# Eight images through two transformer layers: the opening written into each engine's program, and a feed-forward that works in fours

## The chip, the core and the metric

The kernel runs on one core of a Trainium2 chip. A core has five engines with instruction streams of their own, which meet only through semaphores: TensorE (PE in the profile; PEld is its weight load, PEq its sequencer), VectorE (DVE), ScalarE (ACT), GpSimd (POOL) and SyncE (SP, which only starts transfers here). SBUF is the on-chip memory with 128 partitions; PSUM holds eight banks of 512 float32 values per partition, into which PE writes. The metric is the device time of one execution, in microseconds (us).

## The reference

Eight images of 32 x 32 positions and 384 channels go through two layers. B = 8, T = 1024 tokens, C = 384, six heads of 64.

```
x = x + attention0(group_norm(x))          # 32 groups over all positions; scores + rel_h + rel_w,
                                           # from tables rel_pos_h, rel_pos_w; softmax; proj_w, proj_b
t = x as tokens
t = t + causal_attention(layer_norm(t))    # Wq, Wk, Wv, Wo, bo
h = layer_norm(t) @ kron(c_fc_1, c_fc_2).T # 384 -> 1536; c_fc_1 is 1536 x 32, c_fc_2 is 1 x 12
t = t + gelu(h) @ kron(c_proj_1, c_proj_2).T   # c_proj_1 is 32 x 1536, c_proj_2 is 12 x 1
```

Because the feed-forward weights are Kronecker products, the kernel works with 32 values per token: it sums the 384 channels in groups of 12 with c_fc_2, multiplies by c_fc_1 (the up product), takes the gelu, multiplies by c_proj_1 (the down product), and then spreads each of the 32 results over 12 channels with c_proj_2.

## The kernel before

Precision comes from pairs: most operands are split in a high float16 part and a low one, and a product is made of three float16 products (high x high, high x low, low x high). The down and spread products are float32.

**The opening** consists of three blocks of the program. At the end of a block all engines wait for one another.
- `constants` (lines 132 to 277). SP loads four small tables, c_fc_1, c_proj_1, and then eight pieces of weights through five staging buffers. ACT queues six bias loads and the first image (x to `xin`), makes the high half of each weight piece (L182), and later copies tables out of PSUM (L185, L187). DVE makes the low halves (L194). POOL writes every constant in one list of fills (L224) and carvings with affine_select (L230): identities, masks, the group matrix, the position one-hots in `ka0`, zeroed `qc` and `kc`, the spread matrix; each waits for the one before. Only after the last (L265, semaphore `shaped`) does PE start: two products for the relative tables (L272), then 24 transposes of c_proj_1 (L275) and c_fc_1 (L277).
- `first_image`. It normalises image 0: 24 transposes of x in six units (L323), copies on ACT (L328), statistics on DVE, group averages over partitions by PE (`average`, L342, nine products, once for means and once for variances), the root on POOL (L370), the scaled image on ACT (L382), its high half on ACT (L388) and its low half on POOL (L394). PE waits for all six units, then makes the q and k projections, six pairs of heads (`pair_products`, L486). ACT (L505) and DVE (L522, L527) take each pair out of PSUM. POOL then makes twelve turned copies of q (`turn`, L539), which start when the third pair is done.
- The main block, in which each engine runs its own program over the eight images.

**An image in the main block.** PE makes the values (L602, L605), with the relative products between them (L569, 64 rows by 32 columns each, on four column groups), the layer-0 attention, its output projection, the layer norm, the layer-1 projections and attention, the output projection and the feed-forward. During the layer-0 attention the next image is loaded and normalised (L323, L342, L394 between the scores). During the feed-forward PE makes the next image's q and k projections as fill.

**The feed-forward** has twelve steps per image. A step of PE is: `up` (L1218, two products, each 96 rows x 512 columns, into banks 0 and 1), `down` of the step before (L1235, two products with 128 rows and 32 output partitions, at two of four places q), six fill matmuls in steps 1 to 9 (L486), and in steps 7 to 10 a `spread` (L1253, 128 x 384, float32). ACT's gelu (L1226) must be done before the next up, since both use the same banks. ACT also takes out the next image's pairs between gelus (`HIGHS`). After the steps come four more spreads. DVE copies the down sums out (L1241) and adds each spread to x (L1257). SP stores x in two halves (L1263) and loads the next x when both have landed (L1473); POOL adds the output bias to it inside the attention (L997). PE's next values may start at once; its second group of relative products waits for all eight adds.

## Time and profile before

| | us |
|---|---|
| median of 3 runs (lowest, highest) | 3124.77 (3123.82, 3130.79) |
| the profiled execution, its own time | 3126.24 |
| span from its first to its last instruction | 3124.5 |
| PE busy, of the span | 2768.5 (89%) |
| DVE busy | 2187.7 (70%) |
| ACT busy | 1763.3 (56%) |
| POOL busy | 1767.5 (57%) |
| opening, to the first values product | 135.7 |
| image 0 in the main block, to the first values of image 1 | 380.0 |

The busy times are averages over stages with different limits, so the stages have to be read one at a time. A line of a timeline gives the start, the length, the engine, the source line, the instruction, what it writes and reads, how many such instructions are merged in it, and in brackets how long the engine had been idle and what ended that. "issue" is idle time for which no releaser shows.

### The profile page before, as it was taken

The page shows a single profiled execution, that of the slowest core. Times are in us where ns is not written, and L with a number is a line of the kernel's source. Part 1 is how long each engine was busy: PE and PEld are TensorE (multiplying, and loading weights), DVE is VectorE, ACT ScalarE, POOL GpSimd, SP SyncE. Part 2 cuts the span into 40 slices and gives each one's busy share as a digit, 9 for nine tenths or more (in the row PEclk, how much of TensorE's full clock was granted, in tenths as well). Part 3 has the DMA queues.
Part 4 walks back from the last instruction along what each step waited for, and adds up shares of the span by engine and source line. Part 5 has one row for each costly group of instructions (what it writes and reads, how often), then busy time and mean ns, then how long its engine had stood idle before and what let it go on. Part 6 is the DMA issues. An engine that isn't in the chain of part 4 may idle for free.

```text
span 3124.5 us, 68549 instructions
## 1 busy us (share of the span) xinstructions
PE 2768.5 (89%) x29084; PEld 1590.4 (51%) x29084; DVE 2187.7 (70%) x3787; ACT 1763.3 (56%) x2090; POOL 1767.5 (57%) x1166
## 2 busy tenths in 40 slices
PE   1689998999889999899988999989999899889997
PEld 1346563565536554365634556346563565535553
DVE  2476776768768686786857867677776768757684
ACT  2456555566555665565645656556556565555563
POOL 6457373664546656374653737457374574647563
PEclk9799999999999999999999999999999999999998
DMA  2000001000010000100001000100001000010000
GB/s 94 21 21 2 1 2 42 22 2 1 2 62 2 2 2 1 62 2 1 2 11 52 2 1 2 41 22 2 1 2 42 22 2 1 2 42 2 2 2 21
DMA packets 32751, 48.11 MB, mean 15 GB/s; under 512 B 5152, under 2 KB 32032, under 8 KB 32448
## 3 DMA queue, kind: packets, MB, share of 16 engines
q1 hardware_dynamic: 29904, 41.55, 4.0%
q8 instruction: 231, 3.78, 0.5%
q10 hardware_dynamic: 2544, 2.18, 0.2%
q14 instruction: 72, 0.59, 0.1%
HBM read 30.95 MB, written 12.58 MB: 14 GB/s over the span
## 4 chain that ended last, share of the span: by engine, by line
PE 47%; POOL 15%; DVE 15%; issue 12%; ACT 6%; POOLq 0%; DVEq 0%; ACTq 0%
PE ps L486 11%; POOL pl L926 8%; PE ps L812 7%; POOL ph L969 5%; PE ps L602 5%; DVE mxp L882 4%; PE ps L773 4%; PE ps L782 4%; PE ps L737 4%; DVE pl L926 3%; PE ps L1235 3%; PE ps L775 2%; DVE x L1042 2%; DVE stats L1046 2%; PE ps L1253 2%
## 5 line engine op out<-in xcount | busy, mean ns | idle before, releaser
L926 POOL TENSOR_TENSOR pl<-p,ph 128x1024 f16<-128x1024 f32 x336 | 825.2, 2456 | 402.4 <-ACT ph L859 387.4
L882 DVE TENSOR_REDUCE mxp<-ps 128x1 f32<-128x512 f32 (+2 forms) x1344 | 777.8, 626 | 188.7 <-PE ps L737 181.3
L857 ACT ACTIVATE p<-ps 128x1024 f32<-128x1024 f32 (+1 forms) x672 | 644.8, 961 | 450.8 <-PE ps L782 444.6
L812 PEld LDWEIGHTS ps<-v,ph 128*128 128x128 f16 x9600 | 516.6, 98 | 129.5 <-issue 37.6
L926 DVE TENSOR_TENSOR pl<-p,ph 128x1024 f16<-128x1024 f32 (+1 forms) x336 | 414.8, 1234 | 214.4 <-POOL ph L969 212.3
L812 PE MATMUL ps<-v,ph 128*128 128x65 f16 (+1 forms) x9600 | 540.6, 195 | 20.4 <-DVE pl L926 12.5
L812 PE MATMUL ps<-v,pl 128*128 128x65 f16 x4800 | 517.8, 194 | 0.0
L812 PEld LDWEIGHTS ps<-v,pl 128*128 128x128 f16 x4800 | 452.0, 100 | 0.0
L617 POOL TENSOR_TENSOR v<-o,v 128x384 f16<-128x384 f32 x128 | 113.5, 891 | 517.9 <-ACT o L613 517.7
L782 PE MATMUL ps<-qc,kc 65*128 65x512 f16 (+3 forms) x1344 | 388.1, 371 | 0.0
L859 ACT ACTIVATE ph<-p 128x1024 f16<-128x1024 f32 x336 | 355.6, 1058 | 10.7
L969 POOL TENSOR_SCALAR ph<-p 128x1024 f16<-128x1024 f32 (+1 forms) x336 | 331.5, 987 | 0.5 <-ACT p L857 0.2
L773 PE MATMUL ps<-qa,ka 128*128 128x512 f16 x768 | 298.4, 389 | 0.0
L775 PE MATMUL ps<-qb,ka 128*128 128x512 f16 x768 | 298.3, 388 | 0.0
L737 PE MATMUL ps<-ka,qa 128*128 128x512 f16 x768 | 250.4, 387 | 44.3 <-DVE mxp L882 34.6
L782 PEld LDWEIGHTS ps<-qc,kc 65*128 65x128 f16 (+1 forms) x1344 | 126.0, 100 | 131.0 <-issue 9.1
L612 ACT ACTIVATE v<-ps 128x384 f16<-128x384 f32 x128 | 63.7, 498 | 226.3 <-PE ps L605 152.7
L486 PE MATMUL ps<-xin,wqkv_hi 128*128 128x512 f16 x576 | 151.5, 386 | 24.1 <-DVE x L1042 12.4
L737 PE MATMUL ps<-qb,qa 128*128 128x512 f16 (+2 forms) x576 | 157.5, 328 | 15.8 <-DVE mxp L882 15.6
L737 PEld LDWEIGHTS ps<-ka,qa 128*128 128x128 f16 x768 | 73.7, 98 | 188.7 <-DVE mxp L882 90.7
L773 PE MATMUL ps<-qa,qb 128*128 128x512 f16 (+1 forms) x576 | 165.5, 350 | 0.0
L539 POOL TENSOR_SCALAR hT<-qa 64x1024 f16<-64x1024 f16 x48 | 91.5, 1917 | 125.2 <-DVE qc L527 123.5
(182 smaller groups left out, 5300.7 us busy)
## 6 DMA issues: line engine op xcount, KB each, us to landing
x<-in_x SPq DMA_DIRECT2D x8, 1536.0 KB, 7.8
out<-x SPq DMA_DIRECT2D x16, 768.0 KB, 3.8
xin<-in_x SPq DMA_DIRECT2D x7, 1536.0 KB, 6.8
xin<-in_x ACTq DMA_DIRECT2D x1, 1536.0 KB, 19.8
qc<-rowt SPq DMA_DIRECT2D x96, 2.0 KB
o<-in_L_conv_qkv_w SPq DMA_DIRECT2D x2, 576.0 KB, 11.4
p<-in_L_conv_qkv_w SPq DMA_DIRECT2D x1, 576.0 KB, 13.0
x<-in_L_attn_Wq SPq DMA_DIRECT2D x1, 576.0 KB, 13.0
```

The lines of the kernel that those rows point to most:

```text
L486: mm = nc.tensor.matmul(m.ps[:, self.bank[i] + j, :], w[:, k, self.order[i] * P:(self.order[i] + 1) * P], x(k, 4 * j, 4 * j + 4), start=(n ...
L602: mm = nc.tensor.matmul(m.ps[:, 6 + t % 2, 0:C], flat_tile(x(k, t, t + 1)), w[:, k, 2 * C:3 * C], start=(n == 0), stop=(self.layer == 1 an ...
L737: mm = nc.tensor.matmul(m.ps[:, bank, 0:w], m.qa[:, sl, qt * P:(qt + 1) * P], self.ka[:, sl, kh * BANK:kh * BANK + w], start=not diag, sto ...
L773: nc.tensor.matmul(outs[j], self.ka[:, sl, keys[j]], m.qa[:, sl, q], start=True, stop=False)
L775: nc.tensor.matmul(outs[j], self.ka[:, sl, keys[j]], m.qb[:, sl, q], start=False, stop=False)
L782: mm = nc.tensor.matmul(outs[j], m.kc[crows(h), sl, keys[j]], m.qc[crows(h), sl, q], start=False, stop=True)
L812: mm = nc.tensor.matmul(m.ps[:, 6 + half % 2, c0:c0 + w], e, v, start=(first and n == 0), stop=(g in self.last_of_half and n == len(work) ...
L857: nc.scalar.activation(m.p32[:, i % RING, :, 0:w], m.ps[:, 2 * (i % 2):2 * (i % 2) + 2, 0:w], ACT.Exp, scale=SCALE).then_inc(s["exp"], 1)
L859: self.high_part(act, i, lambda out, in_: nc.scalar.activation(out, in_, ACT.Copy), s["hi_act"])
L882: nc.vector.reduce_max(m.mxp[:, h % 2, kh, qt:qt + 1], m.ps[:, bank, 0:w], AX.X).then_inc(s["free"], 1)
L926: engine.tensor_tensor(m.pl[:, i % RING, :, 0:w], m.p32[:, i % RING, :, 0:w], m.ph[:, i % RING, :, 0:w], ALU.subtract).then_inc(sem, 1)
L969: self.high_part(pool, i, lambda out, in_: nc.gpsimd.tensor_scalar(out, in_, 1.0, 0.0, ALU.mult, ALU.add), self.s["hi_pool"])
```

## The change

The blocks of the opening go. A class `Prologue` writes it as one part at the head of each engine's program in the main block, in an order of its own:
- SP loads c_fc_1, c_proj_1, the first image, the small tables, then the weights. The biases stay on ACT's queue.
- POOL makes the identity first, then the group matrix, the small ones and the one-hots for one head of each parity (DVE copies them to the other two later); the 16-bit identities, masks and spread matrix come after the norm's low halves. Zeroing of `qc` and `kc` is cut to the halves that need it and moves to DVE.
- PE transposes c_proj_1 and c_fc_1 first, then x. c_fc_1 goes from PSUM to its place without a copy in SBUF.
- The scaling of the first image moves from ACT to DVE; its low halves are shared by POOL and DVE, and PE starts the first pair channel by channel. Weight halves are put between the steps of ACT and DVE.
- The turned copies are made pair by pair: for image 0, those of the high parts on ACT and those of the low parts on POOL; for later images all on POOL, from the first finished pair on.
- `average` leaves out products of the group matrix whose block is zero: seven products instead of nine, for every image.

The feed-forward works in fours: `down` does four products at the four places q, every second step, behind the fill. The spread matrix becomes 128 x 32 (it sums the four places), so that `spread` gives 32 values per token; it is issued once per half image (after step 8 and at the end). DVE multiplies them out to 384 channels with c_proj_2 (`widen`, two tiles each), and POOL adds the result to x. The next image's values wait for the first two widenings, and its second group of relative products for all four.

```diff
-class Stage:
...
+    def sync(self, sp):
+        d, s = self.d, self.s
+        sp.sem_inc(self.stored, STORES)
+        sp.dma_start(self.c1in, d.c_fc_1.rearrange("(i p) a -> p i a", p=P)).then_inc(s["ffn_in"], 16)
+        sp.dma_start(self.cpin, d.c_proj_1).then_inc(s["ffn_in"], 16)
+        sp.dma_start(self.m.xin[:, :, :], d.x_tiles[0]).then_inc(s["first_in"], 16)
+        for i, r in enumerate((d.rel_h, d.rel_h, d.rel_w, d.rel_w)):
+            sp.dma_start(self.rel2[:, i, :], r).then_inc(s["rel_in"], 16)
+        for i, (src, _, _) in enumerate(self.pieces):
+            if i >= self.NS:
+                sp.wait_ge(s["lo_done"], i - self.NS + 1)
+            sp.dma_start(self.stage[i % self.NS], src).then_inc(self.loads[i % self.NS], 16)
+        sp.wait_ge(s["lo_done"], len(self.pieces))
...
+        act.wait_ge(s["cp_mm"], NF)
+        nc.scalar.activation(m.cp[:, :, :], m.ps[:, 4, 0:NF * FA].rearrange("p (a b) -> p a b", a=NF), ACT.Copy).then_inc(s["cp_out"], 1)
+        act.wait_ge(s["c1_mm"], NF)
+        for r in range(2):
+            nc.scalar.activation(m.c1[r * FA:(r + 1) * FA, :], m.ps[0:FA, 1:4, :].rearrange("p a b -> p (a b)"), ACT.Copy).then_inc(s["c1_hi"], 1)
+        for n in range(2 * NC_):
+            act.wait_ge(norm.s["transposed"], norm.s.at("transposed", n + 1))
+            norm.copy(act, n, n)
+        for i in range(self.NS):
+            self.weight_high(act, i)
+        for n in range(2 * NC_):
+            norm.high(act, n)
+        act.wait_ge(s["biases_in"], 16 * 6)
+        for i in range(2 * NPAIR):
+            if self.NS + i < len(self.pieces):
+                self.weight_high(act, self.NS + i)
+            qkv.pair_high(act, i)
+            if i < NPAIR:
+                for parity in range(2):
+                    act.wait_ge(qkv.s["hi"], qkv.s.at("hi", 2 * i + parity + 1))
+                    dst, src = qkv.turned(0, i, parity)
+                    nc.scalar.activation(dst, src, ACT.Copy).then_inc(qkv.s["turned_hi"], 1)
+        act.wait_ge(s["lo_done"], len(self.pieces))
...
+        dve.wait_ge(s["c1_hi"], 2)
+        nc.vector.tensor_tensor(m.c1[2 * FA:3 * FA, :], m.ps[0:FA, 1:4, :].rearrange("p a b -> p (a b)"), m.c1[0:FA, :], ALU.subtract).then_inc(s["c1_lo"], 1)
+        for n in range(2 * NC_):
+            dve.wait_ge(norm.s["copied"], norm.s.at("copied", n + 1))
+            norm.stats(dve, n, n).then_inc(norm.s["stats"], 1)
+            if n % 2 == 1:
+                dve.wait_ge(norm.s["stats"], norm.s.at("stats", n + 1))
+                norm.aggregate(dve, n // 2)
+        for i in range(2):
+            self.weight_low(dve, i)
+        dve.wait_ge(norm.s["mean_mm"], norm.s.at("mean_mm", 1))
+        norm.mean_out(dve, 6).then_inc(norm.s["mean_out"], 1)
+        dve.wait_ge(norm.s["mean_out"], norm.s.at("mean_out", 1))
+        norm.deviations(dve)
+        self.weight_low(dve, 2)
+        self.weight_low(dve, 3)
+        dve.wait_ge(norm.s["var_mm"], norm.s.at("var_mm", 1))
+        norm.eps(dve, 7).then_inc(norm.s["var_eps"], 1)
+        norm.shifts(dve)
+        dve.wait_ge(norm.s["shift"], norm.s.at("shift", 1))
+        for n in range(2 * NC_):
+            norm.normalise_dve(dve, n)
+            if n % 2 == 1:
+                norm.low_dve(dve, n)
...
+        for i in range(2 * NPAIR):
+            if 4 + i < len(self.pieces):
+                self.weight_low(dve, 4 + i)
+            qkv.pair_low(dve, i)
+        dve.wait_ge(s["ka_made"], 1)
+        for h in (0, 1):
+            for p in (1, 2):
+                nc.vector.tensor_copy(m.ka0[other(h), slot(h) + p, :], m.ka0[other(h), slot(h), :])
...
+        fill(m.ident[:, :], 0.0)
+        carve(m.ident[:, :], ALU.not_equal, 1.0, 0, [[-1, P]], 1, "ident_made")
+        fill(m.group[:, :, :], 1.0 / GC)
...
+        pool.wait_ge(norm.s["var_eps"], norm.s.at("var_eps", 1))
+        norm.root(pool)
+        for n in range(0, 2 * NC_, 2):
+            norm.low(pool, n)
...
+        for i in range(NPAIR):
+            pool.wait_ge(qkv.s["lo"], qkv.s.at("lo", 2 * i + 2))
+            for parity in range(2):
+                qkv.turn(pool, 1, i, parity)
...
+        pe.wait_ge(s["ident_made"], 1)
+        pe.wait_ge(s["ffn_in"], 32)
+        for i in range(NF):
+            nc.tensor.transpose(m.ps[:, 4, i * FA:(i + 1) * FA], self.cpin[:, i * P:(i + 1) * P], m.ident[0:FA, 0:FA]).then_inc(s["cp_mm"], 1)
+        for i in range(NF):
+            nc.tensor.transpose(m.ps[0:FA, 1 + i // 4, (i % 4) * P:(i % 4 + 1) * P], self.c1in[:, i, :], m.ident[:, :]).then_inc(s["c1_mm"], 1)
+        pe.wait_ge(s["first_in"], 16)
+        for n in range(2 * NC_):
+            if n == 1:
+                pe.wait_ge(s["c1_lo"], 1)
+                pe.wait_ge(s["c1_hi"], 2)
+            if n == 4:
+                pe.wait_ge(s["cp_out"], 1)
+            norm.transposes(pe, n, n).then_inc(norm.s["transposed"], 1)
+        pe.wait_ge(s["group_made"], NC_)
+        norm.means(pe, 6).then_inc(norm.s["mean_mm"], 1)
+        norm.variances(pe, 7).then_inc(norm.s["var_mm"], 1)
+        pe.wait_ge(s["anti_made"], 1)
+        pe.wait_ge(s["rel_in"], 64)
+        for i in range(2):
+            nc.tensor.matmul(m.ps[:, 5, i * NREL:(i + 1) * NREL], self.rel2[:, 2 * i:2 * i + 2, :].rearrange("p a b -> p (a b)"), self.anti,
+                             start=True, stop=True).then_inc(s["rel_mm"], 1)
+        pe.wait_ge(s["lo_done"], NC_)
+        for i in range(2 * NPAIR):
+            if i == 1:
+                pe.wait_ge(s["rel_out"], 1)
+            qkv.pair_products(pe, i, channel_ready=norm.ready if i == 0 else None)
+        pe.wait_ge(s["lo_done"], len(self.pieces))
+        pe.wait_ge(s["made"], 1)
+        pe.wait_ge(s["const_dve"], 1)
...
+            near = [k for k in range(NC_) if abs(k - i) <= 1]
+            for k in near:
                 mm = self.nc.tensor.matmul(self.m.ps[:, bank, i:i + 1], self.m.group[:, k, i * P:(i + 1) * P], value(k),
-                                           start=(k == 0), stop=(k == NC_ - 1))
+                                           start=(k == near[0]), stop=(k == near[-1]))
...
+    def turn_all(self, pool):
+        s = self.s
         for p in range(NPAIR):
-            op = self.nc.gpsimd.tensor_scalar(dst[rows, p, :].rearrange("p (w h) -> p w h", w=IMG),
-                                              src[rows, parity * NPAIR + p, :].rearrange("p (h w) -> p w h", h=IMG), 1.0, 0.0, ALU.mult, ALU.add)
-        op.then_inc(self.s["turned"], 1)
-        if n == 3:
-            pool.wait_ge(self.s["turned"], self.s.at("turned", 4))
+            pool.wait_ge(s["lo"], s.at("lo", 2 * p + 2))
+            for part in range(2):
+                for parity in range(2):
+                    self.turn(pool, part, p, parity)
+        pool.wait_ge(s["turned_lo"], s.at("turned_lo", NH))
...
-    BANKS = (6, 6, 6, 6, 0, 1, 0, 1)
-    COUNTS = dict(scaled=8, summed=8, offset=2, x2=8, x2_t=2, x2_hi=4, x2_lo=2, up=12, act=12, each=12, o2=2, spread=8, added=8)
+    BANKS = (6, 0)
+    COUNTS = dict(scaled=8, summed=8, offset=2, x2=8, x2_t=2, x2_hi=4, x2_lo=2, up=12, act=12, each=6, o2=2, spread=2, widened=4, added=8)
...
-    def down(self, pe, i):
+    def down(self, pe, n):
         m, s = self.m, self.s
-        hf, f = i // self.PAIRS, 2 * (i % self.PAIRS)
-        pe.wait_ge(s["act"], s.at("act", i + 1))
-        for j in range(2):
-            q = (f + j) % 4
-            mm = self.nc.tensor.matmul(m.ps[q * FA:(q + 1) * FA, 6 + hf, :], m.cp[:, f + j, :], m.p32[:, i % self.NHID, j, :],
-                                       start=(f + j < 4), stop=(f + j >= NF - 4), skip_group_check=True)
+        hf, f = 2 * n // self.PAIRS, 4 * n % NF
+        pe.wait_ge(s["act"], s.at("act", 2 * n + 2))
+        for q in range(4):
+            mm = self.nc.tensor.matmul(m.ps[q * FA:(q + 1) * FA, 6 + hf, :], m.cp[:, f + q, :], m.p32[:, (2 * n + q // 2) % self.NHID, q % 2, :],
+                                       start=(f == 0), stop=(f == NF - 4), skip_group_check=True)
...
-    def spread(self, pe, t):
-        if t % 4 == 0:
-            pe.wait_ge(self.s["o2"], self.s.at("o2", t // 4 + 1))
-        if t in (1, 2, 3):
-            pe.wait_ge(self.s["added"], self.s.at("added", t))
-        elif t in (4, 5):
+    def spread(self, pe, hf):
+        pe.wait_ge(self.s["o2"], self.s.at("o2", hf + 1))
+        if hf == 1:
             pe.wait_ge(self.s["act"], self.s.at("act", 2 * self.PAIRS))
-        elif t >= 6:
-            pe.wait_ge(self.s["added"], self.s.at("added", t - 1))
-        self.nc.tensor.matmul(self.m.ps[:, self.BANKS[t], 0:C], self.o2[:, t * P:(t + 1) * P], self.m.spread[:, :], start=True, stop=True).then_inc(self.s["spread"], 1)
-    def add(self, dve, t):
-        dve.wait_ge(self.s["spread"], self.s.at("spread", t + 1))
-        self.nc.vector.tensor_tensor(self.m.x[:, t, :], self.m.ps[:, self.BANKS[t], 0:C], self.m.x[:, t, :], ALU.add).then_inc(self.s["added"], 1)
+        for t in range(4 * hf, 4 * hf + 4):
+            mm = self.nc.tensor.matmul(self.m.ps[:, self.BANKS[hf], t % 4 * FA:(t % 4 + 1) * FA], self.o2[:, t * P:(t + 1) * P], self.m.spread[:, :], start=True, stop=True)
+        mm.then_inc(self.s["spread"], 1)
+    def widened(self, n):
+        buf = self.m.ph if n % 2 == 0 else self.m.pl
+        return flat(buf[:, 2:4, :, :].rearrange("p r a b -> p r (a b)")).bitcast(F32)[:, 0:2 * C].rearrange("p (t a b) -> p t a b", t=2, b=FB)
+    def widen(self, dve, n):
+        hf, t = n // 2, 2 * (n % 2)
+        dve.wait_ge(self.s["spread"], self.s.at("spread", hf + 1))
+        if hf == 1:
+            dve.wait_ge(self.s["added"], self.s.at("added", 2 * (n - 1)))
+        y = self.m.ps[:, self.BANKS[hf], t * FA:(t + 2) * FA].rearrange("p (t a) -> p t a", a=FA)
+        self.nc.vector.tensor_tensor(self.widened(n), y.unsqueeze(3).broadcast_to([P, 2, FA, FB]),
+                                     self.m.cp2[:, :].unsqueeze(1).unsqueeze(1).broadcast_to([P, 2, FA, FB]), ALU.mult).then_inc(self.s["widened"], 1)
+    def add(self, pool, n):
+        pool.wait_ge(self.s["widened"], self.s.at("widened", n + 1))
+        x = self.m.x[:, 2 * n:2 * n + 2, :]
+        self.nc.gpsimd.tensor_tensor(x, self.widened(n).rearrange("p t a b -> p t (a b)"), x, ALU.add).then_inc(self.s["added"], 2)
...
+                if before and t == 0:
+                    pe.wait_ge(before.ff.s["widened"], before.ff.s.at("widened", 2))
                 qkv0.v_products(pe, t)
                 for n in WITH_V[t]:
                     if n == 0:
                         pe.wait_ge(qkv0.s["lo"], qkv0.s.at("lo", 2 * PAIRS))
                     if before and n == 1:
-                        pe.wait_ge(before.ff.s["added"], before.ff.s.at("added", NT))
+                        pe.wait_ge(before.ff.s["widened"], before.ff.s.at("widened", 4))
...
-                if i >= 1:
-                    ff.down(pe, i - 1)
                 if i < 2 * ff.PAIRS and FILL[i] and w.next:
                     after.fill(pe, 3 * EACH + sum(FILL[:i]), 3 * EACH + sum(FILL[:i + 1]))
-                if i in SPREADS:
-                    ff.spread(pe, SPREADS.index(i))
-            for t in range(4, NT):
-                ff.spread(pe, t)
+                if i >= 2 and i % 2 == 0:
+                    ff.down(pe, i // 2 - 1)
+                if i == 8:
+                    ff.spread(pe, 0)
+            ff.spread(pe, 1)
...
-            for t in range(4):
-                ff.add(dve, t)
-                if t in (1, 2):
-                    low(4, (t - 1,))
+            low(4, (0,))
+            ff.widen(dve, 0)
+            ff.widen(dve, 1)
+            low(4, (1,))
             low(5, (0,))
             ff.o2_out(dve, 1)
-            ff.add(dve, 4)
-            ff.add(dve, 5)
             low(5, (1,))
-            ff.add(dve, 6)
-            ff.add(dve, 7)
+            ff.widen(dve, 2)
+            ff.widen(dve, 3)
...
-                for n in range(4):
-                    w.next.qkv0.turn(pool, n)
+                w.next.qkv0.turn_all(pool)
+            for n in range(4):
+                ff.add(pool, n)
```

## Rows read from the trace of the kernel before

**Rows 1.** busy time per stage (us): length, then PE, PEld, DVE, ACT, POOL, clock, DMA
```profile
0.00:135.68 135.68, 42.47 (x196) 26.11 (x196) 40.30 (x52) 37.58 (x41) 81.99 (x65) 0.88 0.17 54
...
477.00:515.66 38.66, 37.73 (x140) 11.44 (x139) 14.96 (x18) 19.71 (x19) 22.87 (x12) 0.92 0.06 21
```

**Rows 2.** timeline of the constants, POOL (start us, length us)
```profile
27.19 2.99 POOL L230 TENSOR_SCALAR_AFFINE_SELECT ident<-ident 128x128 f32<-128x128 f32 x2 [0.24 <-POOL kc L224]
...
55.66 0.14 POOL L265 MEMSET small<- 128x48 f32 x1
```

**Rows 3.** the same timeline, weights and feed-forward tables on ACT, DVE, PE
```profile
18.69 1.17 ACT L182 ACTIVATE wqkv_hi<-p 128x1152 f16<-128x1152 f32 x1 [0.86 <-DMA p<-in_L_conv_qkv_w]
...
30.14 1.36 DVE L194 TENSOR_TENSOR wo_lo<-p,wo_hi 128x1152 f16<-128x1152 f32 x1
...
58.32 2.74 PE L277 MATMUL ps<-ident,pl 128*32 128x128 f32 x12
...
61.09 1.44 ACT L187 ACTIVATE lT<-ps 32x1536 f32<-32x1536 f32 x1 [2.18 <-PE ps L277]
...
64.51 1.75 DVE L207 TENSOR_TENSOR c<-lT,c 32x1536 f16<-32x1536 f32 x1
```

**Rows 4.** the same timeline, norm of the first image
```profile
68.52 5.17 PE L323 MATMUL ps<-ident,xin 128*128 128x128 f32 x24 [7.46 <-PEq L132]
...
75.40 2.77 PE L342 MATMUL ps<-gmv,group 128*128 128x1 f32 x18 [1.72 <-DVE gmv L335]
...
79.08 4.00 PE L342 MATMUL ps<-small,group 128*128 128x1 f32 x18 [0.91 <-DVE small L360]
...
84.47 0.81 ACT L382 ACTIVATE hT<-xin,small 128x512 f32<-128x512 f32 x1 [10.15 <-DVE small L374]
...
94.09 1.89 PE L486 MATMUL ps<-xin,wqkv_hi 128*128 128x512 f16 x4 [11.01 <-POOL xin L394]
...
99.74 2.25 ACT L505 ACTIVATE qa<-ps,bqk 64x1024 f16<-64x1024 f32 x2 [6.93 <-PE ps L486]
```

**Rows 5.** timeline, end of the first projections, POOL and PE
```profile
123.71 11.49 POOL L539 TENSOR_SCALAR lT<-qb 64x1024 f16<-64x1024 f16 x6
...
135.73 0.48 PE L602 MATMUL ps<-wqkv_hi,xin 128*128 128x384 f16 x1 [15.68 <-PEq L400]
```

**Rows 6.** DMA issues: times, KB each, median us from issue to landing
```profile
xin<-in_x SPq DMA_DIRECT2D x7, 1536.0 KB, 6.8
xin<-in_x ACTq DMA_DIRECT2D x1, 1536.0 KB, 19.8
```

**Rows 7.** chain of waits in the first feed-forward (start us, length us)
```profile
477.62 1.85 PE ps L1235 x4
...
485.39 0.43 PE ps L1218 x2
485.82 0.98 PE ps L1235 x4
486.81 1.40 PE ps L486 x6
...
506.40 0.65 PE ps L1253 x2
...
514.27 1.56 PE ps L1253 x4
...
517.55 1.13 PE ps L569 x96
518.68 1.57 PE ps L602 x9
```

**Rows 8.** timeline of PE, group means inside the attention
```profile
244.18 2.17 PE L342 MATMUL ps<-gmv,group 128*128 128x1 f32 x18
```

**Rows 9.** one line of POOL: durations ns min, median, max
```profile
L997 POOL TENSOR_TENSOR x<-x,bo x72: 986/994/6696, 184.0 to 2951.5; 128x384 f32<-128x384 f32 x64, 128x3072 f32<-128x3072 f32 x8
```

**Rows 10.** one line of DVE: durations ns min, median, max
```profile
L1257 DVE TENSOR_TENSOR x<-ps,x x64: 548/558/559, 500.2 to 3120.0; 128x384 f32<-128x384 f32 x64
```

352 lines of the change are left out of this document (152 added, 200 removed).

## The prediction

> **What bounds the kernel now.** I read the busy time by stage first, then the timeline of the opening, then the chain of waits through one feed-forward. The first 135.7 us are the opening, once per run: PE works for 42.5 us of it and POOL for 82.0 [rows 1]. The timeline says why. POOL writes every constant in one list and releases PE only after the last one, at 55.8 us, though the identity matrices that the transposes need were carved from 27.2 on, 2.99 for two [rows 2]. Then three blocks run one behind the other: tables, the first norm (from 68.5), the first projections (from 94.1) [rows 4]. The last block ends with POOL's turns, 123.71 + 11.49 = 135.2, and PE, which waited 15.7 us at the block's end, starts the values at 135.73 [rows 5].
>
> After that the bound is PE. In the feed-forward stage of an image with a next one, PE is busy 37.7 of 38.7 us [rows 1], and the chain of waits runs on PE alone: up 0.43, down 0.98, fill 1.40, one after the other, 2.81 a step [rows 7]. What leaves this stage leaves the run, seven times (the eighth image has no fills).
>
> **The opening, step by step.** SP now issues c_fc_1, c_proj_1, x, then the small tables and weights.
> (a) The two feed-forward tables land at about 8 us, and x (issued near 2 us) at about 13. The bounds for x are its landing alone, 6.8 us after issue, and crowded, 19.8 [rows 6]: 9 to 22. I take 13, since the weights now queue behind it.
> (b) PE turns the tables: 2.74 for twelve transposes [rows 3], about 4.2 for all 24 (the other twelve are narrower). ACT copies twice, 2 x 1.44, and DVE subtracts, 1.75 [rows 3]. 8 + 4.2 + 2.9 + 1.8 = 17 us. The second unit of the norm waits for this, so the tables, not x, set the pace. POOL's identity needs only a fill and about 1.4 [rows 2].
> (c) The second unit was at 68.5 + 5.17/6 = 69.4 and the scale was ready at 84.47 [rows 4]: 15.1 us. Each average now has 7 products for 9: 2/9 of 2.77 + 4.00 is 1.5 off. ACT puts five weight halves (1.17 each) and DVE four (1.36 each) between these steps [rows 3]; they fit beside PE's averages except about 1.5. Ready at 17 + 15.1 = 32.
> (d) From the scale to the end of the first pair took 99.74 - 84.47 = 15.3 us, 9.6 of it until all six units were ready [rows 4]. The norm is now split over DVE, ACT and POOL, and the products start channel by channel. I take 10.5: 42.5.
> (e) From there to the values took 135.73 - 99.74 = 36.0 [rows 4, 5]. POOL's turns behind the third pair go: half are POOL's, per pair and in cover of the later pairs, half go to ACT. ACT's load for a q pair is 2.25 + 1.17 + two turns [rows 3, 4]; a turn has 1024 elements as one of the two in the 2.25 has, so 1.1 each, bounded above by POOL's 11.49/6 = 1.9 [rows 4, 5]. That is 5.6 a pair, then three k pairs with PE waiting for banks, about 23 with the last DVE half, and then DVE's four copies, the sum and the bias halves, some 3, while PE waits; with sequencing and bank waits I take 29.5. Values start at 72.
> Saved: 135.7 - 72 = 64. Bounds: 54 (x at 22 costs 5, turns at 1.9 cost 5) to 72 (tables and x sooner by 4, no blocking, 2 less at the end).
>
> **The feed-forward, per image.** Downs: twelve pairs of matmuls at 0.98 [rows 7]. A pair of 128 x 32 products already takes hardly longer than one: it should be near 1.7 one behind the other, as 384 columns of such a product take 0.65 [rows 7] and 512 would take 0.87. Four in four different column groups: nothing in the trace has four with 128 rows. The nearest row is the relative products, which put 96 products of 96 columns on four column groups in 1.13 us, where one by one, at the up's 0.43 for 1024 such columns, they would take 3.9 [rows 7]. So I take 1.0 for a group of four, with 1.97 (two pairs) as the other end: 12 x 0.98 - 6 x 1.0 = 5.8.
> The Trainium skill, TensorE: Matmul & The Clock Gate, section on packing small matmuls, gives 2.38 times for three column tiles rather than 3. By that ratio four would cost about 1.1 and the saving would be 5.2; no row here shows it.
> Spreads: eight of 384 columns, four at 0.65 in the loop and four at 1.56/2 behind it, 5.7 [rows 7]. Now eight of 32 columns. The nearest rows are products of one column, 18 records in 2.17, 0.12 each, two records a product [rows 8]: 8 x 0.24 = 1.9. Upper end the old price. Saved 3.8.
> Given back: behind the shorter loop ACT (gelu and half a high part a step) is late for the last up: the last gelu waits for a high part, and PE idles about 1.6. Net 5.8 + 3.8 - 1.6 = 8.0.
> DVE had eight adds at 0.56 [rows 10], and has four widenings of 768 elements, about 1.0 each, two in the loop, two under the next image's values. The adds go to POOL: 384 elements 0.99, 3072 elements 6.70 [rows 9], so 768 take 1.8. They hide: the turns, 23 us of POOL, start earlier, per pair, and the last two adds lie under the next image's first products; the reload of x comes 2 to 3 us later against those products and is first needed inside the attention. Behind POOL's last adds, which wait for DVE's widening, stand only the value low halves, and PE needs those no sooner than its first weighted values. New waits of PE: the first values for the first two widenings (long done), the second group of relative products for all four, some 2 us behind the spread and under the first values. Uncovered, the last two adds would cost 3.6.
> The clock: at the start of the loop, after PE had waited for the first gelus, a pair of downs ran at 1.85 for 0.98, TensorE's lower level [rows 7]. The new end of the loop has idles of 1.6 and 0.8 with little between them. If it falls there, the next values and relative products (1.57 + 1.13 [rows 7]) take up to 2.4 more. I count half, 1.2: 6.8 net, x 7 = 48. Bounds a image: 2.2 (no four-way overlap) to 9.
> **The averages inside the attention.** Four products fewer per next image, on a PE that does not pause there: 8 records x 0.12 = 0.9 [rows 8], x 7 = 6. If another engine sets the pace there, 0.
> **The last image.** Its steps wait for ACT, so the downs give nothing; four spreads leave the loop (about -2), and the tail gets POOL's adds (1.8 for 0.56, twice): 0, within 3.
>
> **Sum.** 64 + 48 + 6 = 118. Against the profiled execution, 3126.24 (span 3124.5): 3008. The median of the runs, 3124.77, is 1.5 below it, which I leave in the range.
>
> **The rivals.**
> *Four tiles don't overlap.* For it: only pairs are seen with 128 rows. Against: the relative products, 3.5 times faster than one by one. The downs then save nothing: 64 + 7 x 2.2 + 6 = 85, 3041. Chance 0.12.
> *The opening stays serial.* Each engine runs one program in order, so a late weight holds the norm behind it (ACT's copies of five weights ahead of the first high part). If weights (31.5, the end of the last low half [rows 3]), tables 12, norm 24 and projections 30 still add, values start near 98 and it saves 38: 3034. Against it: identity and tables need none of the weights. Chance 0.12.
> *The feed-forward's gain is given back to the next image.* The values now wait for DVE's widening and the stores for POOL. If these take it all: 64 + 6, 3056. Against: DVE works 15.0 of 38.7 us and POOL 22.9 [rows 1]. Chance 0.07.
> *Slower: the clock stays low.* With one down in two steps PE may idle enough to sit at 1.2 GHz for the whole stage. That stage keeps some 30 us of full-speed work, so +30 an image, 210 in all, against 118: 3218. It decides from 118/7 = 17 us an image at the lower level. Against: the fills keep PE at work in nine steps. Chance 0.03.
>
> **How the numbers follow.** The forecast, 3008 (own range 2988 to 3030), has 0.66. I put the range from 2990 to 3042: it takes in the first two rivals and the bounds of the opening. The measurement tells 0.2%, 6 us, from nothing; no case lies within it but a mixture, 0.01. Faster 0.96, slower 0.03.
>
> **What would show it.** The first values near 72 us (right: 62 to 82), x's landing before 14, ACT's turns at 1.1. Four downs in about 1.0 us and not 1.9; spreads at 0.24; a stage, from the second up to the next values, shorter by 6 to 9 us; values at 0.16 us apart (full clock) or 0.32. An image's period shorter by 7 to 8 us. Wrong if x lands past 22, if DVE's ordered list waits on a late weight, or if periods do not shrink.

## The result and the profile after

The changed kernel takes 3034.96 us (median of 4 runs, 3029.49 to 3037.59) against 3127.68 us for the kernel before on the same chip (3123.82 to 3130.79): ratio 0.9702, 95% interval 0.9682 to 0.9721. Its profiled execution took 3037.59 us with a span of 3035.9. I had forecast 3008, with a range from 2990 to 3042: faster as forecast, within the range, 27 us (30 on the profiled execution) short of the forecast itself.

All lines below are of the profiles named, and line numbers are those of the kernel in question; in the changed kernel L327 and L329 are the table transposes, L400 the transposes of x, L501 the low halves of the scaled image, L547 the pairs, L566 their copies on ACT, L583 and L588 on DVE, L205 and L602 the turns on ACT and POOL, L671 the values, L1286, L1302 and L1316 up, down and spread, L1331 the widening and L1337 the wide addition.

Busy time by stage, changed kernel (columns as in [rows 1]); the opening and the first stage with fills:

```profile
0.00:77.34 77.34, 44.31 (x188) 24.81 (x188) 53.05 (x66) 45.27 (x42) 38.01 (x48) 0.86 0.38 116
408.30:446.91 38.61, 32.50 (x167) 12.75 (x166) 23.96 (x24) 26.64 (x27) 26.77 (x14) 0.93 0.06 21
```

The opening is 58.3 us shorter (135.7 to 77.4), with about the same work of PE in it (44.3 against 42.5) and POOL's work down from 82.0 to 38.0. Its timeline, PE, DVE and ACT in turn, against [rows 3 to 5]:

```profile
8.58 1.45 PE L327 MATMUL ps<-ident,p 32*128 32x32 f32 x12 [8.58 <-DMA p<-in_L_ffn_c_proj]
...
14.96 1.11 PE L400 MATMUL ps<-ident,xin 128*128 128x128 f32 x4 [2.25 <-DMA xin<-in_x]
...
17.49 4.26 PE L400 MATMUL ps<-ident,xin 128*128 128x128 f32 x20 [1.41 <-DVE c L216]
...
31.27 0.16 DVE L452 SCALAR_TENSOR_TENSOR small<-small 128x3 f32<-128x3 f32 x1 [1.05 <-POOL small L448]
...
34.60 1.87 PE L547 MATMUL ps<-xin,wqkv_hi 128*128 128x512 f16 x4 [3.54 <-DVE xin L501]
...
41.90 2.24 ACT L566 ACTIVATE qa<-ps,bqk 64x1024 f16<-64x1024 f32 x2 [1.84 <-PE ps L547]
...
44.16 3.91 ACT L205 ACTIVATE hT<-qa 64x1024 f16<-64x1024 f16 x2
...
50.43 1.28 DVE L583 SCALAR_TENSOR_TENSOR qb<-ps,bqk,qa 64x1024 f16<-64x1024 f32 x1 [2.73 <-ACT qa L566]
...
77.39 0.48 PE L671 MATMUL ps<-wqkv_hi,xin 128*128 128x384 f16 x1 [6.65 <-DVE bv L262]
```

Tables at 8.6, second unit at 17.5, scale at 31.3, end of the first pair at 41.9: up to there each mark is within 0.7 us of the forecast (x landed at 15, not 13, ahead of the second unit's turn as assumed). From there to the values it takes 35.5 us instead of 29.5. A turn on ACT takes 1.95, not 1.1, DVE waits 2.7 for ACT behind a pair of them, and at the end PE waits 6.65. The last thing that it waits for are DVE's last constants (2.8 us, from 74.43 to 77.24), which stand behind the low parts of the last pair.

The feed-forward, PE in the changed kernel, against [rows 7]:

```profile
417.59 1.87 PE L547 MATMUL ps<-xin,wqkv_hi 128*128 128x512 f16 x4 [1.39 <-DVE qc L588]
...
435.91 1.06 PE L1302 MATMUL ps<-p,cp 128*32 128x512 f32 x8
436.90 1.08 PE L1316 MATMUL ps<-spread,pl 128*128 128x32 f32 x8
437.82 0.60 PE L1286 MATMUL ps<-ph,c 96*128 96x512 f16 x2
...
443.30 1.07 PE L1302 MATMUL ps<-p,cp 128*32 128x512 f32 x8 [1.43 <-ACT p L1294]
445.18 1.92 PE L1316 MATMUL ps<-spread,pl 128*128 128x32 f32 x8 [0.81 <-DVE pl L1308]
446.91 0.51 PE L671 MATMUL ps<-wqkv_hi,xin 128*128 128x384 f16 x1
```

A float32 product leaves two records, so eight records are four products. Four downs in four column groups take 1.00 (from 435.91 to 436.90, where the spreads start), and a pair of them took 0.98 before. Four spreads take 0.92 at full clock (436.90 to 437.82), 0.23 each, and 1.73 for the last four. Two things are new: a wait of 1.39 in the first fill, for a copy on DVE, and a wait of 1.43 at the last group of downs (the 0.81 behind it was there before). Behind these the granted clock falls to 0.50, the lower level of 1.2 GHz. The first 5 us of the values of the third image, kernel before, then changed (the last three columns are clock, DMA share and GB/s):

```profile
889.00:894.00 5.00, 5.00 (x141) 3.04 (x143) 2.60 (x5) 2.79 (x5) 0.89 (x1) 1.00 0.44 159
```

```profile
818.00:823.00 5.00, 5.00 (x91) 2.86 (x95) 1.82 (x2) 0.87 (x2) 3.67 (x3) 0.50 0.00 0
```

From the start of the values to the first relative product it takes 3.43 us in each of the images 1 to 7 of the changed kernel (counted from 0), and 1.82 in each of them before; the first group of relative products takes 1.7 to 2.1 instead of 1.2.

The table has stage means over the seven images that have a next one (us). The last up and the last down are taken at the start of the last record of each.

| from, to | before | after | forecast |
|---|---|---|---|
| values, first q/k pair of layer 1 | 193.41 | 194.19 | +0.3 (clock +1.2, averages -0.9) |
| from there to the second up | 145.66 | 145.80 | 0 |
| second up, last up | 30.85 | 26.21 | |
| last up, last down | 1.95 | 2.29 | |
| last down, next values | 4.34 | 3.07 | |
| the last three | 37.14 | 31.57 | -8.0 |
| image | 376.22 | 371.57 | -7.7 |

So the account of the spans is: opening -58.3, seven images -32.6 (4.65 each), last image +2.4, together -88.6 with the unrounded numbers (3124.5 to 3035.9). Forecast: -64, -54, 0.

### The profile page after: what moved, and what is told of

It reads as the page before. It is cut to its first block, busy times and chain, and to the rows that moved or that the text cites. A ratio compares the mean times of both kernels' runs of the same rounds, so it can differ in the third digit from the quotient of the medians.

```text
span 3035.9 us, 68416 instructions
## 1 busy us (share of the span) xinstructions
PE 2700.3 (89%) x29020; PEld 1576.3 (52%) x29020; DVE 2223.7 (73%) x3769; ACT 1767.0 (58%) x2091; POOL 1781.9 (59%) x1181
## 4 chain that ended last, share of the span: by engine, by line
PE 42%; DVE 21%; POOL 16%; issue 13%; ACT 7%; DMA 0%; POOLq 0%; DVEq 0%; SPq 0%; ACTq 0%
PE ps L547 10%; POOL pl L995 8%; PE ps L881 6%; POOL ph L1038 5%; DVE mxp L951 5%; PE ps L671 4%; PE ps L842 4%; PE ps L851 4%; PE ps L806 4%; DVE pl L995 3%; ACT qa L655 2%; DVE stats L1115 2%; PE ps L844 2%; DVE x L1111 2%; PE ps L1090 2%
## 5 line engine op out<-in xcount | busy, mean ns | idle before, releaser
L995 DVE TENSOR_TENSOR pl<-p,ph 128x1024 f16<-128x1024 f32 (+1 forms) x336 | 426.5, 1269 | 214.4 <-POOL ph L1038 209.2
L928 ACT ACTIVATE ph<-p 128x1024 f16<-128x1024 f32 x336 | 355.2, 1057 | 10.7
L547 PE MATMUL ps<-xin,wqkv_hi 128*128 128x512 f16 x576 | 158.7, 400 | 32.0 <-DVE qc L588 13.4
L661 DVE TENSOR_TENSOR qb<-ps,qa 32x768 f16<-32x768 f32 x128 | 121.9, 952 | 45.2 <-ACT qa L655 42.4
```

Of the source, the lines that this page charges most:

```text
L547: mm = nc.tensor.matmul(m.ps[:, self.bank[i] + j, :], w[:, k, self.order[i] * P:(self.order[i] + 1) * P], x(k, 4 * j, 4 * j + 4), start=(n ...
L661: self.nc.vector.tensor_tensor(lo, src, hi, ALU.subtract).then_inc(self.s["rel_lo"], 1)
L928: self.high_part(act, i, lambda out, in_: nc.scalar.activation(out, in_, ACT.Copy), s["hi_act"])
L995: engine.tensor_tensor(m.pl[:, i % RING, :, 0:w], m.p32[:, i % RING, :, 0:w], m.ph[:, i % RING, :, 0:w], ALU.subtract).then_inc(sem, 1)
```

## The experiments

The ratios compare each run with the kernel before on the same chip. The spans are those of the profiled executions; "image" is the mean of the seven as in the table above. Images differ by chance: in most kernels one or two of the seven take 3 to 4 us longer somewhere in an attention, so a mean is good to about 1 us (some 7 us of the whole), and a stage that repeats image by image to 0.1. Four kernels whose loop is the changed one (after, h_pool_turns, i_last_adds, k_dve_tail) have means from 370.3 to 371.6.

| run | what it is | ratio to before (95%) | median | span | values start | image | last image |
|---|---|---|---|---|---|---|---|
| before | kernel before | | 3124.77 | 3124.5 | 135.7 | 376.2 | 355.2 |
| after | changed kernel | 0.9702 (0.9682 to 0.9721) | 3034.96 | 3035.9 | 77.4 | 371.6 | 357.5 |
| a_opening | new opening, old loop | 0.9836 (0.9817 to 0.9855) | 3077.7 | 3072.6 | 78.3 | 377.0 | 355.1 |
| b_loop | old opening, new loop | 0.9866 (0.9845 to 0.9886) | 3087.26 | 3084.4 | 125.3 | 371.7 | 357.5 |
| c_averages | before, with the shorter averages | 1.0005 (0.9992 to 1.0018) | 3131.56 | 3127.4 | 134.7 | 376.7 | 355.6 |
| e_v0_early | after, first values before the last downs | 0.9608 (0.9585 to 0.9632) | 3006.57 | 3007.8 | 77.6 | 366.5 | 364.7 |
| f_busy_pe | after, eleven unused products in PE's waits | 0.9642 (0.9617 to 0.9666) | 3015.72 | 3012.9 | 77.9 | 368.6 | 354.9 |
| g_late_turns | after, the loop's turns held back | 0.9615 (0.9589 to 0.9641) | 3007.06 | 2998.0 | 78.7 | 366.6 | 353.4 |
| h_pool_turns | after, the first image's turns all on POOL | 0.9683 (0.9659 to 0.9707) | 3029.9 | 3026.6 | 76.4 | 370.3 | 358.1 |
| i_last_adds | after, the last image's additions on DVE | 0.9697 (0.9675 to 0.972) | 3034.78 | 3032.6 | 77.7 | 371.2 | 356.4 |
| k_dve_tail | after, DVE's last constants earlier | 0.967 (0.9654 to 0.9686) | 3025.81 | 3023.1 | 73.0 | 370.4 | 357.2 |
| n_best | e, g, i and k together | 0.9579 (0.956 to 0.9598) | 2999.23 | 2997.4 | 72.8 | 365.4 | 366.4 |
| p_late_busy | f, g and k together | 0.9591 (0.9575 to 0.9607) | 2998.19 | 2996.5 | 73.2 | 366.6 | 357.4 |
| q_late_tail | g and k together | 0.9598 (0.958 to 0.9617) | 3004.11 | 2998.7 | 72.5 | 366.9 | 357.8 |

### The two parts by themselves

The opening alone: the new prologue on the loop of before.

```
-        constants(nc, ctx, m, d, stored)
...
-        first_image(nc, ctx, m, work[0].norm, work[0].qkv0)
+        prologue = Prologue(nc, ctx, m, d, work[0].norm, work[0].qkv0, stored)
```

> The kernel before with the new opening alone (constants and first norm in each engine's program, seven products an average in the first norm); loop, feed-forward and all later averages as before. Theory 1 (the two parts are independent): the opening gives what it gives in the changed kernel, values start near 77.4 instead of 135.7, 58 us, so about 3067, ratio 0.981; my prediction's figure was 64 (3061, 0.9795). Theory 2 (a part of the 58 us comes back, since the loop's first image then starts at a lower clock or with late turns): values start at 77 but the first image is 3 us or more longer, 3070 or more.

Values start at 78.3, 57.4 us sooner; the whole is 51.9 shorter by the spans and 50.6 by the medians (3077.7 against 3128.3). The missing 5.6 of the span lie in the loop, which is that of before (one image is 6 us longer than its counterpart), and I put them down to chance. So neither theory holds as stated: the total is above the 3067 of theory 1, and the cause that theory 2 gave for that is absent, since the first image is not longer but 4.0 shorter (375.9 against 379.9). In images 1 to 7 the values started at full clock, as in the kernel before:

```profile
830.70:835.70 5.00, 5.00 (x141) 3.04 (x143) 2.60 (x5) 2.79 (x5) 0.89 (x1) 1.00 0.44 156
```

The loop alone: the blocks of the opening are those of before, and all else, also where these blocks use it (spread table, averages, turns pair by pair), is as changed.

```
-        prologue = Prologue(nc, ctx, m, d, work[0].norm, work[0].qkv0, stored)
+        constants(nc, ctx, m, d, stored)
+        first_image(nc, ctx, m, work[0].norm, work[0].qkv0)
```

> The kernel before with its old opening, and the loop of the changed kernel alone (four-block downs and spreads, widening on DVE, adds on POOL, turns started pair by pair, seven products an average). Theory 1 (what the changed trace shows is the loop's own): 32.6 us less over the seven loop stages and 2.4 more in the last image, 30 less, about 3095, ratio 0.990; and the granted clock falls at the start of the values in each image with this opening too. Theory 2 (my prediction's sum for feed-forward and averages was right, and the new opening costs the loop something): 54 us less, about 3071, ratio 0.983, and the clock stays at 1.0 in the values of images 1 to 6.

An image takes 371.7, the last one 357.5, as in the changed kernel, and the clock falls here too:

```profile
870.20:875.20 5.00, 5.00 (x94) 2.86 (x98) 1.82 (x2) 0.87 (x2) 3.69 (x3) 0.50 0.00 0
```

So the loop's part is its own, and the new opening does not cause the fall of the clock. Theory 1 holds but for its total: it gave 41 us by the medians and 40 by the spans, not 30, because the old opening became 10.5 shorter as well (values at 125.3). The first pair starts at 90.4 and not 94.1: x's transposes start 2.7 sooner, which fits the narrower spread table that POOL carves ahead of them, and the shorter averages give 1.0. The turns, now started pair by pair, begin at 100.65 and not 112.01:

```profile
100.65 1.92 POOL L540 TENSOR_SCALAR hT<-qa 64x1024 f16<-64x1024 f16 x1 [10.30 <-DVE qc L526]
```

In the new opening these are there already. Counted twice, the 10.5 make the two parts, 51.9 and 40.1, add up to more than the 88.6 that the change gives, although the 5.6 above work against it.

### The averages alone

```
-            for k in range(NC_):
+            near = [k for k in range(NC_) if abs(k - i) <= 1]
+            for k in near:
```

> The kernel before with one edit: seven products instead of eighteen for each of the two averages, in every image. It tells what the averages are worth by themselves. Theory 1 (the averages lie on TensorE's path in the first head, where the next work waits for them): 0.9 us each of seven images, 6 us, about 3119, ratio 0.998. Theory 2 (TensorE waits for other work there anyway, or one is hidden by the other's copies): nothing, 3125 to 3128, ratio 1.000.

(The "eighteen" above are records: it is seven products for nine.) The averages do get shorter: 14 records in 1.72 where [rows 8] had 18 in 2.17, and from the start of the means to the end of the variances 8.22 instead of 9.11 in all seven images. The whole does not: 12 runs against 17 of before, 1.0005, and the interval excludes the 0.998 of theory 1, so theory 2 holds. From the means to the end of the attention three images take 71.0 for the 72.0 of before; the other four take 72.9 to 74.2. The term is at most a part of 6, and I count it as 0.

### The turns, started earlier

```
     def turn_all(self, pool):
         s = self.s
+        pool.wait_ge(s["lo"], s.at("lo", 2 * NPAIR))
         for p in range(NPAIR):
-            pool.wait_ge(s["lo"], s.at("lo", 2 * p + 2))
```

> The changed kernel, only with the turns of the later images on POOL held back until the low parts of all three q pairs are made, as in the kernel before (in the first image too, whose six POOL turns start later). Theory 1 (the turns that POOL now does beside VectorE's copies lengthen those copies from 0.4 to 0.8 us, and TensorE waits 1.4 us for one in the feed-forward's first fill): the copies are back at 0.4, the 1.4 us wait is gone, and ups of an image take some 25 us instead of 26.2, 5 to 8 us in all against a loss in the opening of some 5 us, whose POOL turns then come last; loop stages 370.5 on average. Theory 2 (the wait has another cause): loop stages unchanged at 371.6, only the opening longer.

The edit reaches only the loop's turns; what I wrote of the first image was wrong, its turns have their own loop in the prologue. The run is 28 us shorter than the changed kernel by the medians and 38 by the spans, much more than expected. The DVE copies of the q pairs in the first feed-forward, changed kernel, and the POOL turns beside them:

```profile
413.23 1.89 POOL L602 TENSOR_SCALAR hT<-qa 64x1024 f16<-64x1024 f16 x1
...
413.69 1.71 DVE L588 COPY qc<-qa 64x1024 f16<-64x1024 f16 x1
...
415.20 1.96 POOL L602 TENSOR_SCALAR lT<-qb 64x1024 f16<-64x1024 f16 x1
...
416.63 0.81 DVE L588 COPY qc<-qa 64x1024 f16<-64x1024 f16 x1
```

and with the turns held back:

```profile
415.60 0.41 DVE L588 COPY qc<-qa 64x1024 f16<-64x1024 f16 x1
...
417.25 0.42 DVE L588 COPY qc<-qa 64x1024 f16<-64x1024 f16 x1
...
422.49 1.90 POOL L602 TENSOR_SCALAR hT<-qa 64x1024 f16<-64x1024 f16 x1 [15.15 <-DVE qc L588]
```

A copy takes 0.41 alone. Beside a turn it waits until the turn has ended: the first starts 0.46 into a turn that ends at 415.12, and is done at 415.40; the second starts 1.44 into a turn that ends at 417.16, and is done at 417.44. All 28 copies of the changed kernel that start within a turn of the loop are done 0.28 to 0.29 after its end, so they last 1.71 or 0.81 by where they meet it. Over the four copies of an image that is some 2.5 of DVE's time. With the turns held back these delays and PE's wait of 1.39 are gone.

Second up to last up takes 23.1 in five of seven images (24.4 in the other two) instead of 25.8 to 26.7. That is 2.7 or more for a wait of 1.39, since behind this wait the clock was low too: 0.66 from 418 to 422 in the changed kernel. And in five of the seven images behind a feed-forward the clock now stays at 1.00 at the start of the values, with 1.8 to the first relative product. An image is 5.0 shorter on the two profiled executions. Theory 1 has the cause right (POOL's turns lengthen the copies, and PE waits for one) and is several times too small.

What counts is which of the two starts first. In the first image of the changed kernel a weight's low half on DVE, whose two inputs are both in SBUF, starts 0.05 us ahead of a turn. It keeps its 1.36, and the turn takes 3.09 for 1.9, done 1.79 after it:

```profile
53.73 1.36 DVE L174 TENSOR_TENSOR wo_lo<-o,wo_hi 128x1152 f16<-128x1152 f32 x1
53.78 3.09 POOL L602 TENSOR_SCALAR lT<-qb 64x1024 f16<-64x1024 f16 x1 [2.33 <-DVE qc L588]
```

The Trainium skill, SBUF — State Buffer, section "SBUF: two separate sides", says that VectorE and GpSimd share a pair of ports, that whichever starts first has it for the whole instruction, and that the other "fully blocks"; it names VectorE's instructions in a 2-port mode and those with two inputs in SBUF. The trace agrees: the copies are done 0.28 after the turn, and the turn 1.79 after the weight's low half. An instruction with one input in PSUM and one in SBUF does not suffer (L583: 1.28 with and without a turn). Which mode the copies run in, no run shows.

### The clock at the start of the values

Eleven products whose result is unused, in PE's two waits at the end of the feed-forward. The wait ahead of them frees the bank that they write; it costs nothing, since last up to last down stays within 0.01 us:

```
                 if i == 2 * ff.PAIRS and w.next:
                     pe.wait_ge(after.s["lo"], after.s.at("lo", 10))
                     for _ in range(7):
                         nc.tensor.matmul(m.ps[:, 2, :], m.wqkv_hi[0][:, 0, 0:P], m.wqkv_hi[0][:, 1, 0:BANK], start=True, stop=True)
...
             if w.next:
                 for _ in range(4):
                     nc.tensor.matmul(m.ps[:, 2, :], m.wqkv_hi[0][:, 0, 0:P], m.wqkv_hi[0][:, 1, 0:BANK], start=True, stop=True)
             ff.spread(pe, 1)
```

> The changed kernel with 11 products added at the end of the feed-forward of each image but the last, 7 before the last group of downs and 4 before the last spreads, 128x512 float16, into a bank that nobody reads then; they are extra work whose result is unused. They fill the two idle pieces of TensorE (1.4 and 0.8 us) and change nothing else. Theory 1 (the granted clock falls because TensorE waits there): values start to first relative product 1.8 us instead of 3.4, first relative group 1.0 instead of 1.5 to 1.8, values to score 33 to 34 instead of 35, an image 1 to 2 us shorter where the added products don't delay the downs, 3023 to 3030. Theory 2 (it falls for something in the loop before, or because of the quarter-width products themselves): clock and times as in the changed kernel, 3035 or up to 1 us an image longer.

```profile
442.67 1.68 PE L1462 MATMUL ps<-wqkv_hi 128*128 128x512 f16 x7
444.27 1.07 PE L1302 MATMUL ps<-p,cp 128*32 128x512 f32 x8
445.27 1.04 PE L1469 MATMUL ps<-wqkv_hi 128*128 128x512 f16 x4
446.15 1.08 PE L1316 MATMUL ps<-spread,pl 128*128 128x32 f32 x8
447.07 0.33 PE L671 MATMUL ps<-wqkv_hi,xin 128*128 128x384 f16 x1
```

More work for PE, and 19 us less by the medians, 23 by the spans. The values start at full clock in all seven images (a value product takes 0.33 and not 0.51, the last spreads 0.92 and not 1.73), the first relative product comes after 1.82, the tail is 2.32 instead of 3.07 and the values' stage 192.1 instead of 194.2. An image is 3.0 shorter, 2.8 of it in these two stages: that is what PE's two waits cost beside their own length. Second up to last up is unchanged (26.3), as it should be. Theory 1 holds; its size, 1 to 2 us an image, was too small.

The same place with useful work: the next image's first values products moved ahead of the last downs.

```
             for t in range(NT - 1):
-                if before and t == 0:
-                    pe.wait_ge(before.ff.s["widened"], before.ff.s.at("widened", 2))
-                qkv0.v_products(pe, t)
+                if not (before and t == 0):
+                    qkv0.v_products(pe, t)
...
+                if i == 2 * ff.PAIRS and w.next:
+                    pe.wait_ge(ff.s["widened"], ff.s.at("widened", 2))
+                    after.v_products(pe, 0)
                 if i >= 2 and i % 2 == 0:
                     ff.down(pe, i // 2 - 1)
```

> The changed kernel with one move: the next image's first values products (128 tokens, 9 matmuls) are issued before the last group of downs of an image and not after its last spreads, so they fill TensorE's 1.4 us of waiting for the last gelu. Theory 1 (waiting of TensorE at the end of the feed-forward, 2.2 us in two pieces, is what the granted clock falls on at the start of the values, and the products also find cover): in images 1 to 6 the stretch from the values' start to the first relative product goes back towards 1.8 us, the first relative group from 1.5 to 1.8 back to 1.0, and an image is 2 to 4 us shorter, 3011 to 3021 in all. Theory 2 (the clock falls for another reason, and the move only fills the waiting): the clock is still 0.5 to 0.6 there, and 1.4 us an image is gained, about 3025.

```profile
442.88 0.33 PE L674 MATMUL ps<-bv,ones 33*128 33x384 f16 x1
443.14 1.07 PE L1302 MATMUL ps<-p,cp 128*32 128x512 f32 x8
445.02 1.08 PE L1316 MATMUL ps<-spread,pl 128*128 128x32 f32 x8 [0.81 <-DVE pl L1308]
```

The 1.43 wait is filled and an image is 5.1 shorter, more than either theory said. But the clock is not whole: it is 1.0 through the spreads and the first relative products, and then falls behind the 0.81 wait and the narrow products, in the next values:

```profile
813.80:818.80 5.00, 5.00 (x113) 2.69 (x111) 4.25 (x5) 4.52 (x7) 4.32 (x4) 0.75 0.30 110
```

The last image is 7 us longer (364.7), as its feed-forward ran at the lower clock throughout (0.50). This happened here and in n_best, for most of it in p_late_busy (0.66 on average) and for a part in b_loop (0.74); the other runs have 0.84 to 0.86. Why was not tried.

### The opening's end

All twelve turns of the first image on POOL:

```
-            if i < NPAIR:
-                for parity in range(2):
...
-                    nc.scalar.activation(dst, src, ACT.Copy).then_inc(qkv.s["turned_hi"], 1)
...
-        for i in range(NPAIR):
...
-                qkv.turn(pool, 1, i, parity)
+        qkv.turn_all(pool)
```

> The changed kernel with all twelve turns of the first image on POOL, none on ScalarE. Theory 1 (ScalarE's six turns of 1.95 us, which I had put at 1.1 each, push back the high parts of the later pairs, and these set the end of the opening): the pairs run 3 to 8 us shorter, values start at 69 to 74 instead of 77.4, unless POOL's row of twelve at 1.9 to 2.5 us from 46 on ends after that (46.5 + 12 x 2.2 = 73). Theory 2 (the opening's end is set by VectorE's low parts and weight parts): values start within 1 us of 77.4, or later because POOL's turns last longer beside VectorE.

Values start at 76.4: taking 11.7 us of turns off ACT gains 1.0. DVE pays for it, since its copies and weight parts now start within turns of POOL's longer row and wait for their ends (0.41 and 1.36 before):

```profile
49.01 0.84 DVE L579 COPY qc<-qa 64x1024 f16<-64x1024 f16 x1
...
51.70 1.96 POOL L593 TENSOR_SCALAR lT<-qb 64x1024 f16<-64x1024 f16 x1
51.93 2.94 DVE L174 TENSOR_TENSOR wo_lo<-o,wo_hi 128x1152 f16<-128x1152 f32 x1
```

Theory 2 holds. The same weight part that went ahead of a turn above, at 1.36, now starts 0.23 behind one and takes 2.94: it is done 1.21 after the turn. So the engine that is freed is paid for by the one that waits for POOL. The run is 5 us shorter by the medians; what is over the 1.0 lies in the loop, which the edit does not touch.

VectorE's last constants (copies of `ka0`, the sum over c_fc_2, the v bias halves), ahead of the last pair's low parts:

```
         for i in range(2 * NPAIR):
             if 4 + i < len(self.pieces):
                 self.weight_low(dve, 4 + i)
+            if i == 2 * NPAIR - 1:
+                dve.wait_ge(s["ka_made"], 1)
...
             qkv.pair_low(dve, i)
```

> The changed kernel with VectorE's last constants of the opening (four copies of ka0, the sum over c_fc_2 and the three v bias steps, 2.9 us) moved ahead of the low parts of the last pair, where VectorE waits 2.7 us for ScalarE. Theory 1 (at the opening's end TensorE waits 6.7 us for these, behind the low parts): values start at 74 to 75 instead of 77.4, when the low parts of the last pair are done, and 72 if nothing but the pairs sets them. Theory 2 (something else, POOL's turns or ScalarE's, ends within 1 us of them): values still start at 76.5 or later. In both cases the first relative products wait for the low parts and turns, so of the gain at the values only what these leave arrives at the first score, 112 us in the changed kernel.

PE's waits from 34 to 78 us (us in total, times, longest), changed kernel:

```profile
PE ps L671 <- DVE bv L262: 6.6, 1, 6.6
PE ps L547 <- DVE qc L588: 4.9, 2, 4.1
```

and in this run:

```profile
PE ps L548 <- DVE qc L589: 5.0, 2, 4.1
...
PE ps L672 <- DVE bv L261: 1.4, 1, 1.4
PE ps L639 <- DVE kc L584: 0.6, 1, 0.6
```

Values start at 73.0, 4.3 sooner, a little more than theory 1 gave, and reach the first relative products with 0.65 of new wait. In the first image the values' stage is 1.8 shorter besides (191.7 against 193.4), at full clock from the start. The whole is 9 shorter by the medians and 13 by the spans; what is over these two lies in the loop, which the edit does not touch.

### The last image's end

```
             ff.widen(dve, 2)
+            if not w.next:
+                ff.add(dve, 2, nc.vector)
             ff.widen(dve, 3)
+            if not w.next:
+                ff.add(dve, 3, nc.vector)
```

(and the same for the first two additions; POOL makes them in the other images only).

> The changed kernel with the last image's four wide additions on VectorE, each right behind its widening, instead of on POOL (the other images as before). Theory 1 (the last image's end, 12.0 us instead of 9.1 before the change, is longer because POOL takes 1.8 us for each of the two additions that come last): the end is 9.5 to 10.5 us, the whole 2 us shorter, 3033. Theory 2 (the widening and the store set it, and POOL's additions lie beside them): the end stays at 12.

The end, from the last down on, is 11.3 instead of 12.0: of 2.9 that the change cost there, 0.7 are POOL's. Changed kernel, then this one:

```profile
3025.29 1.91 PE L1316 MATMUL ps<-spread,pl 128*128 128x32 f32 x8 [0.81 <-DVE pl L1308]
3027.24 0.96 DVE L1331 TENSOR_TENSOR ph<-ps,cp 128x768 f32<-128x768 f32 x1 [2.01 <-PE ps L1316]
3028.12 0.95 DVE L1331 TENSOR_TENSOR pl<-ps,cp 128x768 f32<-128x768 f32 x1
3028.34 1.80 POOL L1337 TENSOR_TENSOR x<-ph,x 128x768 f32<-128x768 f32 x1 [5.20 <-DVE ph L1331]
3030.10 1.80 POOL L1337 TENSOR_TENSOR x<-pl,x 128x768 f32<-128x768 f32 x1
```

```profile
3024.69 0.96 DVE L1331 TENSOR_TENSOR ph<-ps,cp 128x768 f32<-128x768 f32 x1 [2.01 <-PE ps L1316]
3025.75 0.96 DVE L1337 TENSOR_TENSOR x<-ph,x 128x768 f32<-128x768 f32 x1
3026.63 0.95 DVE L1331 TENSOR_TENSOR pl<-ps,cp 128x768 f32<-128x768 f32 x1
3027.68 0.96 DVE L1337 TENSOR_TENSOR x<-pl,x 128x768 f32<-128x768 f32 x1
```

Neither theory holds as stated. The lines suggest where the rest is, but no run shows it: four spreads, two widenings and two additions of 768 now stand one behind the other (1.9 + 3.9), where four short additions followed their own spreads.

### Put together

Held turns, values early, VectorE's tail ahead, last additions on VectorE:

> Four edits on the changed kernel together: the loop's turns held back until the low parts of the q pairs are made, the next image's first values products before the last group of downs, the last image's additions on VectorE, and VectorE's last constants ahead of the last pair's low parts. Theory 1 (they remove separate costs: 3.8 us an image of copies beside POOL's turns, 2 to 2.8 us an image of waiting and low clock at the image's end, 2 at the end, 2 to 3 in the opening): the first two overlap in the clock, which the held turns already keep up in four images of six, so some 364 us a loop stage, 2985, ratio 0.954. Theory 2 (POOL's turns, now last, come into the path once TensorE's waiting is gone, and its wide additions behind them): the values' relative products wait for turns or additions, nothing is gained over held turns alone, 2998 to 3007, ratio 0.960.

Held turns, VectorE's tail ahead, and the eleven added products (unused); and the first two alone:

> Held turns in the loop, VectorE's last constants of the opening ahead of the last pair, and the 11 added products in TensorE's two waits at the end of the feed-forward (their result is unused). Theory 1 (the falls of the clock at the values' start that held turns alone left, in two images of six, are TensorE's waits at the end of the feed-forward): the clock is 1.0 there in all images, the values take 1.8 us to the first relative product, an undisturbed stage is some 363.5 us instead of 365.3, and the opening ends at 73: some 2980 in all. Theory 2 (with the added products the held turns on POOL end too late, and the relative products wait for them): the first relative products come later than 1.8 us, and it takes 2995 or more.

> Held turns in the loop and VectorE's last constants of the opening ahead of the last pair, nothing else: the plain candidate. If the two add up, the span is 2998.0 of the held turns less 4 to 5, some 2993, and the median some 3000; if the opening's gain is lost again in the first image, 2998.

All three lie where the held turns alone lie (span 2998.0): 2997.4, 2996.5, 2998.7. In n_best the feed-forward has 23.1 and a negative tail, but with the values early the relative products come while POOL still turns:

```profile
436.25 1.08 PE L1317 MATMUL ps<-spread,pl 128*128 128x32 f32 x8 [0.81 <-DVE pl L1309]
438.07 0.22 PE L639 MATMUL ps<-qa,rel_hi 64*32 64x96 f16 x2 [0.74 <-POOL lT L603]
```

Behind these two waits the clock fell again: in e_v0_early, where the relative products find their turns made, the first score comes 36.2 after the first values product, here 38.5. The last image's feed-forward ran at 0.50 here too. Theory 2 holds. In p_late_busy the clock was 1.00 at the start of the values in all seven images, as theory 1 said; its total was not, 2996 and not 2980: an image takes 364.3 to 366.3 where little disturbs it, but three took 367.8 to 368.6, and in the last image most of the feed-forward was at 0.50. In q_late_tail the clock fell in three images of seven, and its span is the 2998 of the second case that I had named. So what the opening and the clock give over held turns shows in their own stages and is lost in the scatter of the rest. The best medians, 2998 and 2999, are 36 us below the changed kernel, and 28 of these come with one line, held turns (3007); the intervals of these four kernels overlap, so more than that is not shown.

## Why the prediction was right, point by point

- **The opening, (a) to (d).** Right: tables before x, second unit 17.5 (17 forecast), scale 31.3 (32), first pair 41.9 (42.5). It did not stay serial, and that rival falls.
- **The opening, (e).** The term that was too small: 35.5 for 29.5. ACT's turn was priced at 1.1, from the half of a copy out of PSUM; it takes 1.95, my upper bound, and six of them make 5.1 more. But that is not simply what it cost: taken off ACT they gave 1.0, as DVE then waited for POOL's turns. The other item of this step, "some 3, while PE waits", was sized right, 2.8, but misplaced: DVE stood idle for 2.7 ahead of the last low parts, and with the constants moved there the values start 4.3 sooner. How the missing 6.0 divide between the two is not shown. Saved 58.3 for 64, within the bounds 54 to 72.
- **The downs and spreads.** Right: a group of four at 1.00, so 12 x 0.98 - 6 x 1.00 = 5.8; a spread 0.23 for 0.24. The first rival, that four tiles do not overlap, falls. By the ratio for three tiles of the Trainium skill, TensorE: Matmul & The Clock Gate, section "Part 3: Packing small matmuls — row/col tiling", it would by estimate have been 1.1; the trace has 1.00.
- **Given back.** The wait at the last gelu is 1.43 for the 1.6 forecast. With held turns an undisturbed image takes 27.7 from the second up to the next values (three of seven), against 36.1 in four of the seven images before: 8.3 for the 8.0 of my sum. So the terms of the feed-forward's products were right; what is missing is in the step below.
- **The base.** Image 0, whose rows I read, takes 39.1 for this stage, with the clock low at the loop's start; the mean of the seven is 37.1. My 8.0 is a sum of terms at full clock and does not depend on this. But measured against image 0 alone the stage would seem 7.5 shorter, and against the mean it is 5.6.
- **The step that failed: "They hide: the turns, 23 us of POOL, start earlier, per pair".** I costed the earlier start at nothing because POOL was free. DVE's copies waited for the ends of POOL's turns, a copy was late for the first fill, PE waited 1.39, and the clock was low behind it. Held turns take 5.0 us an image off on the profiled executions, and 28 in all by the medians: 3007, within 1 of the forecast. That it meets it so closely is partly luck, as the opening fell 6 short and the averages gave nothing for 6.
- **The clock.** Counted at half, 1.2 an image. It fell in all images, and cost some 2.8 with the last spreads and the slower values' stage. Five of seven falls went with the held turns, all with PE's waits filled. So the clock and the turns are in part the same 5 us.
- **The averages.** 0.9 in their own stretch, 0 in the total, the end that I had named "if another engine sets the pace there, 0". Which engine takes it was not tried.
- **The last image.** 0 within 3, measured +2.4.
- **Giving back to the next image.** In small this rival is true: by the clock. Its own mechanism, waits for the widening or the additions, is not there; PE waits for neither.

Open: why the third image takes 1.8 to 6 us longer than the one ahead of it, from its values to the projections of layer 1, in ten of the eleven kernels with the new opening and in none of the three with the old; what puts the last feed-forward at the lower clock in some of them; and why, behind the same two waits (1.43 and 0.81), the clock falls in two images of g_late_turns and not in the other five. With the turns not held it fell in 34 of 35 images (the changed kernel, b_loop, h_pool_turns, i_last_adds, k_dve_tail); the exception is one image of i_last_adds. So two short waits alone do not settle it.

## What to carry to other kernels

Before an engine's work is started earlier because that engine is free, look at what runs beside it: VectorE's copies within SBUF waited for the end of GpSimd's, and TensorE waited for those. Which of the two starts first decides which one waits. At the end of a dense stretch price TensorE's waits at more than their length, here 2.2 us of waiting cost 2.8 more, and try filling them, with useful work if there is some that does not bring its own waits along. And measure a loop stage over several rounds of the loop, not by the first.

## What was unexpected of the hardware

- Four float32 products of 128 rows, 32 columns of weights and 512 moving columns, in four column groups, take 1.00 us together; two take 0.98.
- A DVE copy of 64 x 1024 float16 within SBUF (0.41 alone) that starts during a POOL copy is done 0.28 after that one's end, 28 times of 28, and so takes 0.81 or 1.71. A DVE subtraction of 128 x 1152 with both inputs in SBUF (1.36 alone) is done 1.21 after it and takes 2.94; started 0.05 ahead of the POOL copy it keeps its 1.36, and the POOL copy takes 3.09 for 1.9. One that reads PSUM and SBUF takes 1.28 in all cases.
- A strided float16 copy of 64 x 1024 takes ACT 1.95, as it takes POOL 1.9, though ACT reads 64 x 1024 of float32 out of PSUM in 1.11.
- Eleven added products made the kernel 19 us faster.
